# A selective scan: the input of four of 16 states added on TensorE, and C applied by diagonals

## The chip, the cores and the metric

The kernel runs on one core of a Trainium2 chip. The metric is the time of one execution in device microseconds (us). The page and the trace come from one profiled execution. TensorE shows as PE (its weight loads as PEld), VectorE as DVE, ScalarE as ACT, GpSimd as POOL, SyncE's DMA queue as SPq.

## The reference

A decoder layer: a selective state space scan (with convolution, gate and projections), cross attention and a quantized feed-forward net, each with a residual and a layer norm. The change lies in the scan, which runs over eight steps of 128 independent rows, with 512 channels and 16 states:

```python
def step(h, inp):
    d_t, u_t, B_t, C_t = inp
    dA = jnp.exp(d_t[..., None] * A)
    h = dA * h + (d_t * u_t)[..., None] * B_t[:, None, :]
    y = jnp.einsum('bdn,bn->bd', h, C_t)
    return (h, y)
_, ys = jax.lax.scan(step, h0, (deltas, us, Bs, Cs))
y = (ys + us * D[None, None, :]) * _silu(zs)
out = jnp.einsum('md,lbd->lbm', out_proj_w, y)
```

Everything is f32 here. B and C have one value for each row and state, D one for each channel.

## The kernel before

The work is written out by hand for each engine, with semaphores between them. A set-up (about 83 us) makes projections, the convolution, softplus and the skip products: for these, jobs UD multiply blocks of U by `diag_d`, diagonal matrices of D, in true f32 matmuls (128x128 weights, 128 columns, 16 in a burst). Jobs Z are f32 matmuls with 512 columns. Then comes the scan, steps t = 0 to 7 (until about 234 us), and then the attention with the net, on TensorE for the most part.

In the scan the 128 rows lie on partitions, so a state of a step is a tile of 128x512 in `H`. Each of steps 1 to 6 runs through 16 states n:

- GpSimd multiplies delta by A for two states at a time (L1155, a ring of four buffers).
- ScalarE (`decay`, L932) takes the exponential into a PSUM bank of a ring of four (`RING`), once the state four places earlier has left the bank.
- VectorE (`state_decay`, L1355) multiplies the bank by the old state, and `state_add` (L1362) adds B times the input (`step_du`) and writes the new state to `H`. It starts the product of state n+1 ahead of the addition of state n.
- ScalarE (`weigh`, L940) multiplies the state by C, row by row, into one of four slots of `hc` (`WRING`), three states behind the decay (`BEHIND`).
- TensorE (`state_sum`, L574) turns the four 128x128 blocks of the slot (transposes against an identity) and adds them up over states in PSUM bank 4. So the sum over states is done while turning, and Y is kept channel by row.

Ahead of a step's sums `skip_sum` turns the step's skip product into the same bank. It has to wait until `gate` (VectorE, after state 3 of the next step, L1370) has read the last step's Y. After state 3 TensorE projects the gated Y of the step before (`out_proj`), after state 11 it turns x1, the normed result (`turn_x1`). VectorE's `norm1_stats` and `norm1` stand after states 9 and 11. After states 4, 8, 12 and 15 TensorE does a side job, which makes weights of the attention: 22 in all, of the kinds P (four), KV (two), N (four), M (eight: four 128x128 matmuls each) and R (four). ScalarE takes their results some states later (`take_side`, after states 11 and 15 and, of the next step, 2 and 6). Step 7 does without `H` as a target: VectorE (`last_state`, L1398) weighs with C directly into `hc`. When step 7's norm of the token tile before and its decays are through, SyncE loads the attention's rope tables (L423) to where A had been.

Of the kernel before, what the change touches and what calls it, by code (L numbers as in the profile page):

```python
# [21 lines left out]
ACT = mybir.ActivationFunctionType  # L22
AX = mybir.AxisListType

P = 128
T = 8
DM = 256
DI = 512
NST = 16
# [13 lines left out]
RING = 4  # L43
WRING = 4
MRING = 2 * (DM + DQ)
BEHIND = 3
FRESH = 3
PE_SIDE = (4, 8, 12, 15)
ACT_SIDE = (11, 15, NST + 2, NST + 6)
G = 4  # L50
# [27 lines left out]
def decoder_layer(nc, x_fm, x_tiles, wx, wz, conv_w, w_xp, w_dt, b_dt, a_log, d_skip, w_out,  # L78
                  w_q, w_kcq, w_qr, w_kr, w_kckv, w_o, ctx_kv, w_up, w_dn,
                  ident_c, rope_q, rope_kv, had, out, zs_dram, ud_dram, x1_dram, a_dram):  # L80
    with ExitStack() as stack:
# [84 lines left out]
        bcT = x_t[:, :]  # L166
        diag_d = ud_t[:, :].rearrange("p (c n) -> p c n", c=CI)
        wup_raw, wdn_raw = kvT[:, :, :].rearrange("p t n -> p (t n)"), hc[:, 2:4, :].rearrange("p s d -> p (s d)")
        ctx_s = yT[:, :, :].rearrange("p c n -> p (c n)").rearrange("p (t d) -> p t d", t=T)

        Abc = reg_a[:, 0:NST * DI].rearrange("p (n d) -> p n d", n=NST)
# [1 line left out]
        dA = reg_b[:, 8192:12288].rearrange("p (b n d) -> p b n d", b=RING, n=SA)  # L173
        delta_r = reg_c[:, 0:4096].rearrange("p (t d) -> p t d", t=T)
        du_r = reg_c[:, 4096:8192].rearrange("p (t d) -> p t d", t=T)

        ropeq_s = reg_a[:, 0:1536].rearrange("p (w a c n) -> p w a c n", w=2, a=2, c=QC)
        had_s = reg_a[:, 1536:1536 + P]
# [43 lines left out]
        dve_passed = sem("dve_passed"); pool_passed = sem("pool_passed"); act_passed = sem("act_passed"); pe_passed = sem("pe_passed")  # L222

        arg_s = sem("arg_s"); da_s = sem("da_s"); dah_s = sem("dah_s"); h_s = sem("h_s")
        cb_s = sem("cb_s"); hc_s = sem("hc_s"); yl_s = sem("yl_s"); y_s = sem("y_s"); udm = sem("udm")
        st_x = sem("st_x"); st_z = sem("st_z"); st_u = sem("st_u")
        y2_s = sem("y2_s")
# [81 lines left out]
        def work_of(t):  # L309

            return last_work if isinstance(t, int) and t == T - 1 else loop_work

        def last_slot(n):
            return (n + 1 + int(n > FRESH)) % WRING
# [135 lines left out]
        def _(pe):  # L450
# [10 lines left out]
            for j, job in enumerate(jobs):  # L461
# [51 lines left out]
                elif kind == "TU":  # L513
                    once(ld["consts"], 16)
                    for i in range(2):
                        t = 2 * c + i
                        for k in range(CI):
                            last = pe.transpose(o[:, i, k * P:(k + 1) * P], U[:, k, t * P:(t + 1) * P], ident[:, :])
                last.then_inc(pe_job, 1)
            pe.wait_ge(dve_free, freed[("TU", T // 2 - 1)][1])  # L520

            def side_job(j):
# [54 lines left out]
            def skip_sum(t, Y=ps[:, 4, :]):  # L577
# [5 lines left out]
                    last = turn_onto(Y[:, c * P:(c + 1) * P], ud_t[:, c * P:(c + 1) * P], c == 0 and t < T - 1, False)  # L583
                last.then_inc(udm, 1)

            def state_sum(slot, done, count, last_state, Y=ps[:, 4, :], first_state=False):

                pe.wait_ge(done, count)
                for c in range(CI):
                    last = turn_onto(Y[:, c * P:(c + 1) * P], hc[:, slot, c * P:(c + 1) * P], first_state and c == 0, last_state)  # L590
                last.then_inc(y_s, 1)
# [20 lines left out]
            state_sum(0, hc_s, 1, True)  # L612
            pe.wait_ge(ld["wout"], 16)
            for t in range(1, T - 1):
                skip_sum(t)
                for n in range(NST):
                    state_sum((n + 1) % WRING, hc_s, NST * (t - 1) + n + 2, n == NST - 1)
                    if n in PE_SIDE:
                        side_job(per_step * (t - 1) + PE_SIDE.index(n))
                    if n == 3:  # L620
                        out_proj(t - 1)
                    elif n == 11:
                        turn_x1(t - 1)
# [218 lines left out]
        def _(act):  # L842
# [77 lines left out]
            def decay(t, n):  # L920


                act.wait_ge(arg_s, AG * (t - 1) + n // SA + 1)
                if t == T - 1 and n >= RING:
                    act.wait_ge(yl_s, n + 1 - RING)
                else:
                    need(act, h_s, NST * (t - 1) + n + 1 - RING)
                if t == 1 and n == 0:
                    act.wait_ge(act_free, freed[("Z", CI - 1)][1])
                if t == 1 and n == 2:  # L930
                    act.wait_ge(dve_free, freed[("TU", T // 2 - 2)][1])
                act.activation(ps[:, n % RING, :], dA[:, n // SA % RING, n % SA, :], ACT.Exp,  # L932
                               scale=-1.0).then_inc(da_s, 1)

            def weigh(t, n):

                act.wait_ge(h_s, NST * (t - 1) + n + 1)
                need(act, y_s, NST * (t - 1) + n + 2 - WRING)
                s = NST + n
                act.activation(hc[:, (n + 1) % WRING, :], H[:, n, :], ACT.Copy,  # L940
                               scale=bc[:, t, s:s + 1]).then_inc(hc_s, 1)

            squares_of(0)
            skips(0)
# [60 lines left out]
            def scan_step(t, carried):  # L1005
                for n in range(NST):
                    decay(t, n)
                    if n >= BEHIND and t < T - 1:
                        weigh(t, n - BEHIND)
                    elif n < BEHIND and carried:  # L1010
                        weigh(t - 1, NST + n - BEHIND)
                    if t == T - 1 and n == FRESH + 2:
                        fresh_share()
                    if n in ACT_SIDE:
                        take_side(per_step * (t - 1) + ACT_SIDE.index(n))
                    if carried and NST + n in ACT_SIDE:
                        take_side(per_step * (t - 2) + ACT_SIDE.index(NST + n))
                take_x1(t - 1)
# [214 lines left out]
        def _(dve):  # L1233
# [112 lines left out]
            def state_decay(t, n):  # L1346

                dve.wait_ge(da_s, NST * (t - 1) + n + 1)
                E_n = ps[:, n % RING, :]
                if isinstance(t, int) and t == 1:  # L1350

                    dve.scalar_tensor_tensor(E_n, E_n, step_b(0, n), step_du(0), ALU.mult,  # L1352
                                             ALU.mult).then_inc(dah_s, 1)
                    return
                dve.tensor_tensor(E_n, E_n, H[:, n, :], ALU.mult).then_inc(dah_s, 1)  # L1355

            def state_add(t, n):

                dve.wait_ge(dah_s, NST * (t - 1) + n + 1)
                if not (isinstance(t, int) and t == 1):  # L1360
                    dve.wait_ge(hc_s, NST * (t - 2) + n + 2)
                dve.scalar_tensor_tensor(H[:, n, :], step_du(t), step_b(t, n), ps[:, n % RING, :], ALU.mult,  # L1362
                                         ALU.add).then_inc(h_s, 1)

# [28 lines left out]
            def last_state(n):  # L1393

                dve.wait_ge(da_s, NST * (T - 2) + n + 1)
                dve.wait_ge(hc_s, NST * (T - 3) + n + 2)
                dve.wait_ge(y_s, NST * (T - 2) + 1 + n + int(n > FRESH) - WRING + 1)
                dve.scalar_tensor_tensor(hc[:, last_slot(n), :], ps[:, n % RING, :], step_b(T - 1, NST + n), H[:, n, :],  # L1398
                                         ALU.mult, ALU.mult).then_inc(yl_s, 1)

# [10 lines left out]
            def scan_step(t):  # L1411
                state_decay(t, 0)
                for n in range(NST):
                    if n < NST - 1:
                        state_decay(t, n + 1)
                    state_add(t, n)
                    if n == 3:
                        gate(t - 1)
                    elif n == 9:
                        norm1_stats(t - 1)  # L1420
                    elif n == 11:
                        norm1(t - 1)
# [273 lines left out]
```

## Time and profile before

| | us |
|---|---|
| median of three runs | 492.42 (491.68 to 494.4) |
| profiled execution | 493.22 |
| its span, first to last instruction | 491.4 |
| TensorE busy | 415.2 |
| VectorE busy | 390.7 |
| ScalarE busy | 296.8 |
| GpSimd busy | 215.7 |

Busy times are sums over stages with different limits, so the scan is read by itself: by the table of stretches (busy time of each engine between two times, with the clock that was granted to TensorE, 1.00 for 2.4 GHz and 0.50 for 1.2 GHz), by the order of time on single engines, and by who waited for whom. In the order of time a row joins like instructions that follow each other; its start, its busy time and the count stand first. From the start of one row to the start of the next is the time that a group takes when nothing waits. A busy time has the last matmul's way through the array in it, which overlaps the next group. A true f32 matmul leaves two records, a turn one.

### The profile page before, as it was taken

The numbers are of one execution on the slowest core, as the hardware profiler recorded it, in microseconds if no ns is written. First come the engines' busy times: TensorE is split into PE (matmuls) and PEld (weight loads), VectorE is DVE, ScalarE is ACT, GpSimd is POOL, SyncE is SP. The second block draws the span as 40 slices with busy tenths as digits, with TensorE's granted clock in tenths as the row PEclk, the third lists the DMA queues.
The fourth block names the chain that finished last, engine by engine and source line by source line (L and its number), as shares of the span: only waits on it lengthen the run. The fifth ranks groups of instructions, "written<-read, shape, count | busy, mean of one in ns | idle before, by whom it ended". The sixth has DMA issues, their size and how long they took to land.

```text
span 491.4 us, 11537 instructions
## 1 busy us (share of the span) xinstructions
PE 415.2 (84%) x4148; PEld 341.4 (69%) x4148; DVE 390.7 (80%) x744; ACT 296.8 (60%) x699; POOL 215.7 (44%) x157
## 2 busy tenths in 40 slices
PE   4978973587886977969999999999999999999853
PEld 1435532556675866958888888988888888888642
DVE  1876869999999999998466477879878787987675
ACT  3635997899999999995034445453554545354530
POOL 2400003997979797987333332331424233132101
PEclk9989995598798998799999999999999999999955
DMA  8970373116210241101400000000000000000000
GB/s 280 379 302 3 127 226 107 53 43 144 84 53 18 72 158 45 36 29 36 143 1 4 1 13 1 12 13 12 11 0 21 0 11 11 11 11 0 23 1 22
DMA packets 18659, 30.94 MB, mean 63 GB/s; under 512 B 2113, under 2 KB 11713, under 8 KB 17921
## 3 DMA queue, kind: packets, MB, share of 16 engines
q1 hardware_dynamic: 18624, 30.49, 18.8%
q8 instruction: 21, 0.34, 0.3%
q14 instruction: 14, 0.11, 0.1%
HBM read 24.16 MB, written 6.32 MB: 62 GB/s over the span
## 4 chain that ended last, share of the span: by engine, by line
PE 55%; DVE 18%; ACT 14%; issue 9%; DMA 2%; POOL 1%; DVEq 0%; SPq 0%; POOLq 0%; ACTq 0%
PE ps L452 46%; ACT hc L940 5%; PE ps L574 4%; DVE reg_b L1362 4%; PE ps L688 3%; ACT ps L932 3%; DVE ps L1355 2%; DVE ps L1352 2%; DVE reg_b L1296 2%; DVE reg_b L1249 1%; DMA xw<-x_fm 1%; ACT reg_b L912 1%; DMA reg_a<-rope_q 1%; ACT reg_b L1036 1%; POOL reg_b L1155 1%
## 5 line engine op out<-in xcount | busy, mean ns | idle before, releaser
L1155 POOL TENSOR_TENSOR reg_b<-reg_c,reg_a 128x1024 f32<-128x1024 f32 x56 | 130.5, 2373 | 60.4 <-DVE reg_c L1301 60.3
L1178 POOL TENSOR_TENSOR reg_b<-reg_b 128x768 f32<-128x768 f32 x32 | 57.9, 1810 | 117.0 <-DVE reg_b L1434 117.0
L452 PE MATMUL ps<-x1T,Mw 128*128 (+1 forms) x768 | 93.1, 278 | 1.1 <-DVE reg_b L1434 1.1
L452 PEld LDWEIGHTS ps<-x1T,Mw 128*128 128x128 f32 x768 | 88.3, 192 | 3.9 <-DVE reg_b L1434 1.8
L574 PE MATMUL ps<-ident,hc 128*128 128x128 f32 x456 | 72.7, 309 | 16.6 <-ACT hc L940 15.3
L574 PEld LDWEIGHTS ps<-ident,hc 128*128 128x128 f32 x456 | 59.3, 159 | 27.1 <-ACT hc L940 23.9
L940 ACT ACTIVATE hc<-reg_b,bc 128x512 f32<-128x512 f32 x96 | 68.8, 717 | 6.9 <-DVE reg_b L1362 3.4
L1362 DVE SCALAR_TENSOR_TENSOR reg_b<-reg_c,bc,ps 128x512 f32<-128x512 f32 x96 | 70.8, 742 | 0.0
L932 ACT ACTIVATE ps<-reg_b 128x512 f32<-128x512 f32 x112 | 65.8, 592 | 6.9 <-POOL reg_b L1155 6.1
L1355 DVE TENSOR_TENSOR ps<-ps,reg_b 128x512 f32<-128x512 f32 x80 | 55.3, 697 | 0.1
L1036 ACT ACTIVATE reg_b<-ps,small 128x128 f32<-128x128 f32 x128 | 45.3, 373 | 12.8 <-DVE small L1439 12.8
L1160 POOL TENSOR_TENSOR small<-small 128x1 f32<-128x1 f32 x24 | 13.2, 549 | 80.5 <-DVE small L1380 80.5
L452 PE MATMUL ps<-reg_b 64*64 64x128 f32 (+1 forms) x768 | 40.9, 274 | 3.8 <-ACT reg_b L1043 0.5
L1043 ACT ACTIVATE reg_b<-ps 128x512 f32<-128x512 f32 x32 | 19.1, 598 | 40.7 <-PE ps L688 40.7
L452 PEld LDWEIGHTS ps<-reg_b 64*64 64x64 f32 (+1 forms) x768 | 29.4, 134 | 11.2 <-issue 10.2
L1433 DVE TENSOR_TENSOR reg_b<-ps,reg_a 128x768 f32<-128x768 f32 x32 | 30.6, 955 | 7.4 <-PE ps L452 4.8
L452 PE MATMUL ps<-xw,Nw 128*128 128x512 f32 x64 | 30.4, 635 | 6.9 <-DMA xw<-x_fm 6.9
L452 PE MATMUL ps<-reg_b,Nw 64*64 64x128 f32 x1024 | 35.3, 275 | 0.3 <-POOL reg_b L1178 0.2
L1049 ACT ACTIVATE reg_b<-ps 128x256 f32<-128x256 f32 x32 | 12.3, 386 | 33.3 <-PE ps L452 33.3
L452 PEld LDWEIGHTS ps<-reg_b,Nw 64*64 64x64 f32 x1024 | 27.6, 132 | 5.7 <-issue 4.8
L1434 DVE TENSOR_TENSOR reg_b<-ps,reg_a 128x768 f32<-128x768 f32 x32 | 30.3, 948 | 0.0
L452 PE MATMUL ps<-Pw,reg_b 128*128 128x256 f32 x128 | 29.9, 382 | 0.5 <-ACT reg_b L1049 0.5
(150 smaller groups left out, 677.3 us busy)
## 6 DMA issues: line engine op xcount, KB each, us to landing
reg_a<-a_dram SPq DMA_DIRECT2D x4, 1024.0 KB, 7.8
Mw<-w_o SPq DMA_DIRECT2D x1, 2048.0 KB, 15.9
ud_dram<-reg_b SPq DMA_DIRECT2D x4, 512.0 KB, 4.0
zs_dram<-x1T SPq DMA_DIRECT2D x4, 512.0 KB, 3.7
ud_t<-ud_dram SPq DMA_DIRECT2D x8, 256.0 KB, 2.8
zs_t<-zs_dram SPq DMA_DIRECT2D x8, 256.0 KB, 2.7
xw<-x_fm SPq DMA_DIRECT2D x2, 512.0 KB, 5.7
mring<-w_q SPq DMA_DIRECT2D x4, 256.0 KB, 3.8
```

Source lines behind the costliest of these rows:

```text
L452: return pe.matmul(o, l, r, start=start, stop=stop)
L574: return pe.matmul(o, src, ident[:, :], start=start, stop=stop, is_transpose=True, skip_group_check=True)
L932: act.activation(ps[:, n % RING, :], dA[:, n // SA % RING, n % SA, :], ACT.Exp, scale=-1.0).then_inc(da_s, 1)
L940: act.activation(hc[:, (n + 1) % WRING, :], H[:, n, :], ACT.Copy, scale=bc[:, t, s:s + 1]).then_inc(hc_s, 1)
L1036: last = act.activation(prob[:, g % 2, h, :], scores_at(k)[:, h % 2, h // 2, :], ACT.Exp, bias=negm[:, g % 2, h:h + 1], accum_out=sums[:, ...
L1043: act.activation(probT[:, g % 2].rearrange("p h n -> p (h n)"), turned, ACT.Copy).then_inc(pte, 1)
L1155: pool.tensor_tensor(dA[:, g % RING], delta_r[:, bass.ds(t, 1), :].to_broadcast([P, SA, DI]), Abc[:, g * SA:(g + 1) * SA, :], ALU.mult).th ...
L1178: pool.tensor_tensor(rq[:, g % 2].rearrange("p a c n -> p (a c n)"), pc[:, g % 2].rearrange("p a c n -> p (a c n)"), psn[:, g % 2].rearran ...
L1355: dve.tensor_tensor(E_n, E_n, H[:, n, :], ALU.mult).then_inc(dah_s, 1)
L1362: dve.scalar_tensor_tensor(H[:, n, :], step_du(t), step_b(t, n), ps[:, n % RING, :], ALU.mult, ALU.add).then_inc(h_s, 1)
L1433: dve.tensor_tensor(pc[:, g % 2], v, ropeq_s[:, 0], ALU.mult)
L1434: dve.tensor_tensor(psn[:, g % 2, ::-1], v, ropeq_s[:, 1], ALU.mult).then_inc(ropem, 1)
```

## The change

For states 1, 3, 9 and 12 (`ON_PE`) in steps 1 to 6, VectorE makes the product alone. TensorE adds the input onto the product in its PSUM bank (`add_input`): one f32 matmul with a diagonal of B as weights and the step's input, 512 columns, moving. ScalarE makes that diagonal (`diagonal_b`, 128x128) and copies the state from PSUM to `H` (`take_state`). Ahead of the scan TensorE writes each of the three banks concerned once, with the identity.

For all 16 states of these steps C is applied on TensorE: ScalarE makes a diagonal of C (`diagonal`, 128x128 from the identity) in place of the weighed state, and `weighed_sum` multiplies the four blocks of `H` by it, four true f32 matmuls in place of four turns. The 16 diagonals fill all of `hc`. The sums run in another order (`SUM_ORDER`), the projection stands after state 5, and the four additions stand at the step's start (1, 3) and after the sums of states 7 and 10. A state in `H` may be overwritten only when its sum is done, so VectorE's additions, ScalarE's copies and diagonals wait for the sum of the step before (`y_s`). Step 7 starts its weighing when the sums of step 6 that use its slots are done.

```diff
...
+ON_PE = (1, 3, 9, 12)
+SUM_ORDER = (0, 2, 4, 1, 5, 6, 3, 7, 8, 10, 11, 9, 13, 14, 12, 15)
+ADDS = NST - len(ON_PE)
...
+        diag_c = hc[:, :, :].rearrange("p s (i n) -> p (s i) n", n=P)
...
+        diag_b = delta_r[:, 0, :].rearrange("p (i n) -> p i n", n=P)
...
+            pe.wait_ge(cst, 3)
+            pe.wait_ge(act_free, freed[("Z", CI - 1)][1])
+            for b in sorted({n % RING for n in ON_PE}):
+                if b >= 2:
+                    pe.wait_ge(dve_free, freed[("TU", T // 2 - 2)][1])
+                for c in range(CI):
+                    last = mm(ps[:, b, c * P:(c + 1) * P], identb[:, :], identb[:, :], c == 0, c == CI - 1)
+                last.then_inc(set_s, 1)
...
+            def add_input(t, n):
+                pe.wait_ge(dah_s, NST * (t - 1) + n + 1)
+                pe.wait_ge(db_s, on_pe(t, n))
+                pe.matmul(ps[:, n % RING, :], diag_b[:, ON_PE.index(n), :], du_r[:, t, :], start=False, stop=True,
+                          skip_group_check=True).then_inc(pa_s, 1)
+            def weighed_sum(t, n, Y=ps[:, 4, :]):
+                pe.wait_ge(hc_s, NST * (t - 1) + n + 2)
+                new_state(pe, t, n)
+                for c in range(CI):
+                    last = pe.matmul(Y[:, c * P:(c + 1) * P], H[:, n, c * P:(c + 1) * P], diag_c[:, n, :],
+                                     start=False, stop=n == NST - 1, skip_group_check=True)
+                last.then_inc(y_s, 1)
...
             for t in range(1, T - 1):
+                add_input(t, 1)
+                add_input(t, 3)
                 skip_sum(t)
-                for n in range(NST):
-                    state_sum((n + 1) % WRING, hc_s, NST * (t - 1) + n + 2, n == NST - 1)
+                for n in SUM_ORDER:
+                    weighed_sum(t, n)
+                    if n == 7:
+                        add_input(t, 9)
+                    elif n == 10:
+                        add_input(t, 12)
                     if n in PE_SIDE:
                         side_job(per_step * (t - 1) + PE_SIDE.index(n))
-                    if n == 3:
+                    if n == 5:
                         out_proj(t - 1)
                     elif n == 11:
                         turn_x1(t - 1)
...
-                    need(act, h_s, NST * (t - 1) + n + 1 - RING)
+                    u, m = (t, n - RING) if n >= RING else (t - 1, n - RING + NST)
+                    if u >= 1:
+                        new_state(act, u, m)
+                if t == 1 and n < RING:
+                    act.wait_ge(set_s, sum(b <= n for b in {m % RING for m in ON_PE}))
...
-            def weigh(t, n):
-                act.wait_ge(h_s, NST * (t - 1) + n + 1)
-                need(act, y_s, NST * (t - 1) + n + 2 - WRING)
+            def diagonal_b(t, n):
+                i = ON_PE.index(n)
+                need(act, pa_s, on_pe(t - 1, n))
+                act.activation(diag_b[:, i, :], ident[:, :], ACT.Copy, scale=bc[:, t, n:n + 1]).then_inc(db_s, 1)
+            def take_state(t, n):
+                act.wait_ge(pa_s, on_pe(t, n))
+                if t > 1:
+                    act.wait_ge(y_s, summed(t - 1, n))
+                act.activation(H[:, n, :], ps[:, n % RING, :], ACT.Copy).then_inc(ev_s, 1)
+            def diagonal(t, n):
+                if t == 1 and n == 0:
+                    act.wait_ge(y_s, 1)
+                if t > 1:
+                    act.wait_ge(y_s, summed(t - 1, n))
                 s = NST + n
-                act.activation(hc[:, (n + 1) % WRING, :], H[:, n, :], ACT.Copy,
-                               scale=bc[:, t, s:s + 1]).then_inc(hc_s, 1)
+                act.activation(diag_c[:, n, :], ident[:, :], ACT.Copy, scale=bc[:, t, s:s + 1]).then_inc(hc_s, 1)
...
                     decay(t, n)
-                    if n >= BEHIND and t < T - 1:
-                        weigh(t, n - BEHIND)
-                    elif n < BEHIND and carried:
-                        weigh(t - 1, NST + n - BEHIND)
+                    if t < T - 1:
+                        if n + 1 in ON_PE:
+                            diagonal_b(t, n + 1)
+                        diagonal(t, n)
+                        if n - RING + 1 in ON_PE:
+                            take_state(t, n - RING + 1)
...
+                if n in ON_PE:
+                    dve.wait_ge(ev_s, on_pe(t - 1, n))
                 dve.tensor_tensor(E_n, E_n, H[:, n, :], ALU.mult).then_inc(dah_s, 1)
...
-                    dve.wait_ge(hc_s, NST * (t - 2) + n + 2)
+                    dve.wait_ge(y_s, summed(t - 1, n))
                 dve.scalar_tensor_tensor(H[:, n, :], step_du(t), step_b(t, n), ps[:, n % RING, :], ALU.mult,
                                          ALU.add).then_inc(h_s, 1)
...
                 dve.wait_ge(da_s, NST * (T - 2) + n + 1)
-                dve.wait_ge(hc_s, NST * (T - 3) + n + 2)
-                dve.wait_ge(y_s, NST * (T - 2) + 1 + n + int(n > FRESH) - WRING + 1)
+                if n in ON_PE:
+                    dve.wait_ge(ev_s, on_pe(T - 2, n))
+                dve.wait_ge(y_s, NST * (T - 2) + 1 + max(n + int(n > FRESH) - WRING + 1, min(0, n - 2)))
...
                 for n in range(NST):
                     if n < NST - 1:
                         state_decay(t, n + 1)
-                    state_add(t, n)
+                    if n not in ON_PE:
+                        state_add(t, n)
```

TensorE's order in step 2, before, from the skip sum on (`ud_t` the skip product, `hc` the weighed states, `w_out_s` the projection, `x_t` the residual, `Mw` with `ident` a side job KV):

```order
L574 MATMUL ps<-ident,ud_t 128x128 x4
L574 MATMUL ps<-ident,hc 128x128 x16
L452 MATMUL ps<-w_out_s,yT 128x256 x4
L574 MATMUL ps<-ident,x_t 128x128 x2
L574 MATMUL ps<-ident,hc 128x128 x4
L533 MATMUL ps<-ident,Mw 128x128 x4
```

The same place now (`reg_c` with 512 columns the additions, `hc,reg_b` the diagonals of C against the states):

```order
L624 MATMUL ps<-reg_c 128x512 x2
L608 MATMUL ps<-ident,ud_t 128x128 x4
L632 MATMUL ps<-hc,reg_b 128x128 x12
L567 MATMUL ps<-ident,Mw 128x128 x4
L632 MATMUL ps<-hc,reg_b 128x128 x8
L478 MATMUL ps<-w_out_s,yT 128x256 x4
L608 MATMUL ps<-ident,x_t 128x128 x2
L632 MATMUL ps<-hc,reg_b 128x128 x12
L624 MATMUL ps<-reg_c 128x512
L632 MATMUL ps<-hc,reg_b 128x128 x4
```

Two additions stand ahead of the skip sum, the projection has moved behind five sums and a side job, and every sum is a group of matmuls against `reg_b`, the states.

VectorE's order around the gate in the loop over steps, before: the product of state 4, then the addition of state 3, then the gate (`yT`).

```order
L1355 TENSOR_TENSOR ps<-ps,reg_b 128x512 [waits da_s]
L1361 REGISTER_ALU [waits dah_s]
L1362 ISA [waits hc_s]
L1362 SCALAR_TENSOR_TENSOR reg_b<-reg_c,bc,ps 128x512
L1368 REGISTER_ALU [waits y_s]
L1370 TENSOR_TENSOR yT<-ps,zs_t 128x512 [waits op_s,st_z]
```

The same place now, from the addition of state 2 on:

```order
L1440 ISA [waits y_s]
L1440 SCALAR_TENSOR_TENSOR reg_b<-reg_c,bc,ps 128x512
L1424 REGISTER_ALU
L1433 TENSOR_TENSOR ps<-ps,reg_b 128x512 [waits da_s]
L1446 REGISTER_ALU [waits y_s]
L1448 TENSOR_TENSOR yT<-ps,zs_t 128x512 [waits op_s,st_z]
```

The addition of state 3 is gone, so the gate follows the product of state 4 directly, and additions wait for `y_s`, the sums, where they waited for `hc_s`.

## Rows read from the trace of the kernel before

**Rows 1.** The page, busy time of each engine over the span.

```profile
PE 415.2 (84%) x4148; PEld 341.4 (69%) x4148; DVE 390.7 (80%) x744; ACT 296.8 (60%) x699; POOL 215.7 (44%) x157
```

**Rows 2.** Stretches of the scan: steps 2 and 3, and the start of step 1.

```profile
core 0: us, PE busy (x) PEld busy (x) DVE busy (x) ACT busy (x) POOL busy (x), PEclk, DMA share, GB/s
...
114.18:136.26 22.08, 18.53 (x137) 16.12 (x137) 21.89 (x38) 20.53 (x39) 18.88 (x10) 0.77 0.39 105
136.26:158.33 22.07, 16.70 (x144) 13.98 (x145) 21.88 (x38) 21.42 (x44) 19.25 (x10) 0.92 0.13 36
...
91.57:96.00 4.43, 4.43 (x21) 4.43 (x22) 4.43 (x8) 3.38 (x7) 4.43 (x3) 0.50 0.18 59
```

**Rows 3.** VectorE's order of time in step 3: start, busy time, line.

```profile
138.62 0.70 DVE L1355 TENSOR_TENSOR ps<-ps,reg_b 128x512 f32<-128x512 f32 x1
139.22 0.74 DVE L1362 SCALAR_TENSOR_TENSOR reg_b<-reg_c,bc,ps 128x512 f32<-128x512 f32 x1
139.88 0.70 DVE L1355 TENSOR_TENSOR ps<-ps,reg_b 128x512 f32<-128x512 f32 x1
```

**Rows 4.** TensorE's waits in the scan: total us, times, longest.

```profile
PE ps L574 <- DVE yT L1370: 15.0, 5, 6.0
```

**Rows 5.** TensorE's order of time in step 5, nothing waiting.

```profile
180.86 1.91 PE L574 MATMUL ps<-ident,hc 128*128 128x128 f32 x16
182.61 1.89 PE L452 MATMUL ps<-w_out_s,yT 128*128 128x256 f32 x8
...
184.56 0.60 PE L574 MATMUL ps<-ident,hc 128*128 128x128 f32 x4
184.99 1.06 PE L452 MATMUL ps<-mring 128*128 128x128 f32 x8
185.89 2.17 PE L574 MATMUL ps<-ident,hc 128*128 128x128 f32 x16
```

**Rows 6.** TensorE's order of time in the set-up: jobs UD, Z, UD.

```profile
45.15 3.74 PE L452 MATMUL ps<-ud_t,reg_b 128*128 128x128 f32 x32
48.72 7.03 PE L452 MATMUL ps<-xw,Nw 128*128 128x512 f32 x16
55.59 3.73 PE L452 MATMUL ps<-ud_t,reg_b 128*128 128x128 f32 x32
```

**Rows 7.** TensorE's order of time: side jobs P, N and R.

```profile
98.92 1.08 PE L452 MATMUL ps<-Mw 128*64 128x256 f32 x8
...
140.97 1.12 PE L452 MATMUL ps<-Mw 64*64 64x64 f32 x24
...
164.62 1.90 PE L452 MATMUL ps<-mring 128*128 128x64 f32 x16
```

**Rows 8.** Groups of ScalarE in the scan: busy us, mean ns, idle before.

```profile
L940 ACT ACTIVATE hc<-reg_b,bc 128x512 f32<-128x512 f32 x96 | 68.8, 717 | 6.9 <-DVE reg_b L1362 3.4 <-PE ps L574 3.0
L932 ACT ACTIVATE ps<-reg_b 128x512 f32<-128x512 f32 x112 | 65.8, 592 | 6.9 <-POOL reg_b L1155 6.1 <-DVE hc L1398 0.7
...
L986 ACT ACTIVATE Nw<-ps,small 128x128 f32<-128x128 f32 x8 | 2.5, 368 | 0.0
```

**Rows 9.** The scan's end, in order of time: TensorE, VectorE, SyncE's queue, VectorE.

```profile
220.15 5.24 PE L574 MATMUL ps<-ident,hc 128*128 128x128 f32 x32 [0.48 <-ACT hc L940]
...
231.91 0.54 DVE L1390 TENSOR_SCALAR x<-ps,small 128x256 f32<-128x256 f32 x1
...
232.91 0.37 SPq L423 DMA_DIRECT2D reg_a<-rope_q  x1
...
234.51 0.69 DVE L1370 TENSOR_TENSOR yT<-ps,zs_t 128x512 f32<-128x512 f32 x1 [0.75 <-PE ps L574]
...
237.50 0.96 DVE L1433 TENSOR_TENSOR reg_b<-ps,reg_a 128x768 f32<-128x768 f32 x1 [2.30 <-DMA reg_a<-rope_q]
```

**Rows 10.** TensorE's order of time at the start of step 1.

```profile
92.45 3.62 PE L574 MATMUL ps<-ident,hc 128*128 128x128 f32 x16
```

**Rows 11.** TensorE's order of time, start of the attention.

```profile
239.38 2.94 PE L452 MATMUL ps<-x1T,Mw 128*128 128x128 f32 x24 [0.28 <-DVE reg_b L1434]
```

More of the change, by code:

```diff
@@ L224, in decoder_layer @@
         arg_s = sem("arg_s"); da_s = sem("da_s"); dah_s = sem("dah_s"); h_s = sem("h_s")
+        db_s = sem("db_s"); set_s = sem("set_s"); pa_s = sem("pa_s"); ev_s = sem("ev_s")
         cb_s = sem("cb_s"); hc_s = sem("hc_s"); yl_s = sem("yl_s"); y_s = sem("y_s"); udm = sem("udm")
@@ L311, in work_of, with summed, added, on_pe @@
             return last_work if isinstance(t, int) and t == T - 1 else loop_work
+        def summed(t, n):
+            return NST * (t - 1) + SUM_ORDER.index(n) + 2
+        def added(t, n):
+            return ADDS * (t - 1) + sum(m not in ON_PE for m in range(n + 1))
+        def on_pe(t, n):
+            return len(ON_PE) * (t - 1) + ON_PE.index(n) + 1
+        def new_state(eng, t, n):
+            if n in ON_PE:
+                eng.wait_ge(ev_s, on_pe(t, n))
+            else:
+                eng.wait_ge(h_s, added(t, n))
         def last_slot(n):
@@ L1395, in last_state @@
                 dve.wait_ge(da_s, NST * (T - 2) + n + 1)
-                dve.wait_ge(hc_s, NST * (T - 3) + n + 2)
-                dve.wait_ge(y_s, NST * (T - 2) + 1 + n + int(n > FRESH) - WRING + 1)
+                if n in ON_PE:
+                    dve.wait_ge(ev_s, on_pe(T - 2, n))
+                dve.wait_ge(y_s, NST * (T - 2) + 1 + max(n + int(n > FRESH) - WRING + 1, min(0, n - 2)))
                 dve.scalar_tensor_tensor(hc[:, last_slot(n), :], ps[:, n % RING, :], step_b(T - 1, NST + n), H[:, n, :],
```

## The prediction

> **What bounds the kernel now.** The page first: TensorE is busy for 84% of the span and VectorE for 80% [rows 1], which says little, because the kernel has two halves with different limits. The table of stretches, cut at TensorE's skip sums, gives the scan by steps [rows 2]; steps 2 and 3 stand there for the six. VectorE is busy for 21.89 of 22.08 us and 21.88 of 22.07 us. ScalarE has 20.5 and 21.4, GpSimd 18.9 and 19.3, TensorE 18.5 and 16.7, drawn out by waits. So VectorE paces steps 1 to 6. In VectorE's own order of time a decay product starts 0.60 us before the addition behind it, and that 0.66 us before the next product [rows 3]: 1.26 us a state, 20.2 us for 16, which leaves 1.9 us a step for the gate and the layer norm. TensorE is idle for lack of input: its longest waits are those of the skip sum for the gate, 15.0 us in five [rows 4].
>
> **What the change takes away.** Four of 16 additions leave VectorE: 4 x 0.66 = 2.6 us a step, so VectorE alone could do a step in 19.4 us, and GpSimd's 19 us [rows 2] stand close behind. Over six steps that is up to 15.9 us. That is the gain, if nothing else is late.
>
> **What it puts on TensorE.** Three prices are needed, all at the full clock and back to back, from start to start.
> - A state's sum before: four turns (transposes) in 184.99 - 184.56 = 0.43 us [rows 5]; the row of 16 agrees, 1.75 us to the next.
> - A state's sum after: four true f32 matmuls of 128x128 with 128 columns, the state as weights and a diagonal moving. The kernel has this very shape in its set-up: the skip products multiply U by a diagonal of D. Sixteen of them (32 records, two for each matmul) take 48.72 - 45.15 = 3.57 us [rows 6], so 0.223 each and 0.89 us for four. A second place: a weight product of four matmuls in the scan takes 185.89 - 184.99 = 0.90 us [rows 5].
> - An addition of the input: one f32 matmul with 512 columns. Eight of these took 55.59 - 48.72 = 6.87 us [rows 6]: 0.86 us each.
>
> In a step TensorE then has 16 x 0.89 = 14.3 (before 16 x 0.43 = 6.9), additions 4 x 0.86 = 3.4 (before none), the skip sum 0.43, the output projection with its two turns 184.56 - 182.61 = 1.95, the turn of x1 in two turns, half of 0.43, 0.22: 20.3 us. To this come the side jobs, not changed: about 1.0 for one of P or N (1.08 and 1.12 busy, with a tail that overlaps what follows), 1.74 for R (1.90 busy less the same 0.16 by which the rows of M exceed 0.90) [rows 7], 0.90 for M, 0.43 for KV with its four turns. By steps (four P; two KV, two N; two N, two M; two R, two M; three M, one R; one M, one R) 4.0, 2.9, 3.8, 5.3, 4.4 and 2.6: 23.0. A step is so 22.9 to 25.6 us of TensorE work with no gap. That is above the 22.0 of now and far above VectorE's 19.4: **TensorE becomes the bound**, and the four additions bought from VectorE are paid twice, by the additions (3.4 us a step) and, more, by the diagonals of C (7.4 us a step).
>
> A rule on the same point: the Trainium skill, "TensorE: Matmul & The Clock Gate", section Terms, calls transpose mode four times faster for FP32. By it a sum would cost 4 x 0.43 = 1.7 us instead of 0.89. Here rows show a factor of 2 [rows 5, 6]; what that rule would give in time stands among the rivals.
>
> **What can be hidden, and what waits.** Within a step TensorE is rarely short of input. Behind the skip sum it has states 0 and 2 ready, VectorE makes a state in 1.26 us or 0.6 for one of the four, and TensorE takes 0.89 for each plus about 9 us of other work spread between, so it falls behind and stays behind. ScalarE: each 512-wide weighing (717 ns) becomes a 128-wide diagonal, nearest row the 128x128 copy with a scale, 368 ns [rows 8]. With 16 decays at 592, 20 diagonals at 368, four evictions of states at about 592 and some 3 us of jobs that is 22 us without overlap; before, the same count gives 24 where 20.5 to 21.4 were busy. So I take about 19 us for ScalarE, by the row nearest to a diagonal. Were a diagonal as dear as the weighing that it replaces (717), ScalarE would come to 29 by that count and to some 25 with the overlap, level with TensorE; were it free, nothing would change, since TensorE is the bound.
>
> The place to look at is the end of a step. The gate waits for the last sum, and the skip sum waits for the gate; now two additions (1.7 us) stand between, which were not there to fill the 15 us [rows 4]. But ScalarE evicts the job behind state 12 before decay 3: eviction 0.59, decay 0.59, diagonal 0.37, decay 0.59, then VectorE's product 0.70 [rows 3] and the gate 0.69 [rows 9] are 3.5 us, and with the hand-overs I take 4.0, against the last sum, a job and the two additions on TensorE, 0.89 + 1.0 + 1.7 = 3.6. I take 0.4 us of wait at each of the four boundaries whose last job is short: 1.6 us. Bounds: 0 where every hand-over is short (R is long enough to cover it), 1 us each where ScalarE also evicts the two-part N.
>
> The new wait on ScalarE, state 1's eviction on its addition, has decay 5 queued behind it; that holds VectorE until about 2.9 us into the step, when TensorE is still at states 0 and 2 with a skip sum ahead. The diagonals wait for the sum of the step before, which is done by then.
>
> The clock. At the start of step 1 the granted clock is 0.50, so 1.2 GHz, until 96 us [rows 2]; before it the engine had been idle. There 16 turns took 3.62 us where 1.91 stand later [rows 5, 10]. TensorE does in 4.4 us what it could in 2.2: +2.2 us for step 1. Later steps hold few gaps, so I take 2.4 GHz; bounds are 0 and another 4.4 us.
>
> **The sum.** 6 x 20.3 + 23.0 = 144.8; less the first step's two early additions, which lie before its skip sum, 1.7; plus 2.2 and 1.6: 146.9 us from the first skip sum. That starts at about 91.2 (the gate stands behind two additions fewer, but GpSimd paces those first states), so the last sum of step 6 ends at 238.1. Before, it ended at 220.15 + 0.66 = 220.8 [rows 9]. So +17.3. Behind it, the rope tables are loaded once the norm of token tile 6 is through: norm 231.91, load 232.91, used at 237.50, 16.7 us after the last sum [rows 9]. In the new order VectorE starts the last step while two sums are open and is not held by GpSimd, which had time to fill its four buffers: 12 products at the 0.66 of an addition [rows 3] and the 1.9 of gate and norm make 9.8, so the norm is done 9.9 us after the last sum, load half a microsecond later, 4.6 to its use: 15.0, so -1.7. In all +15.6. The profiled execution took 493.22 us for its span of 491.4; it becomes 508.8, and as it stood 0.8 above the median of the runs, the time is **508 us**.
>
> Bounds: the sum at 0.98 for four matmuls, as 24 records in 2.94 us at the start of the attention would have it [rows 11], adds 96 x 0.09 = 8.4; boundaries and clock at their worst add about 4. All of the small terms at zero take off 3.8, and a shorter tail 1.5. So 503 to 520.
>
> **Rivals.**
> - The gain arrives: TensorE's two-record matmuls of different sums overlap better than in the set-up, VectorE stays the bound, and a step takes 19.4 us: 493 - 6 x 2.6 = 477 us. For that a TensorE step of 20.3 + 3.8 (the mean of the jobs) has to fall to 19.4, so a sum from 0.89 to 0.60 us. At 0.76 the step is the 22 us of now, and from there on the change is slower; the set-up's diagonals at 0.89 speak against both. Chance 0.03, and 0.03 for the level case (490 to 495).
> - TensorE bound, but the boundary is bare: gate 2 us late at five boundaries, and each gap drops the clock as in step 1, 5 x (2 + 2.2) = +21, so about 529. For it: the clock now falls in the middle of the scan, mean 0.77 in the second step [rows 2]. Against: the gaps that did so are those the two additions fill. Chance 0.12.
> - A sum at four times a turn (the mechanism of transposes in one pass against four): 96 x (1.72 - 0.89) = +80, about 588. Chance 0.02, since the set-up rows show half of that price. The rule of the Trainium skill named above, in "TensorE: Matmul & The Clock Gate" (Terms), is this case.
> - The forecast: 0.80.
>
> **How the numbers follow.** Predicted 508; the range 503 to 520 holds most of the forecast and the mild part of the bare boundary. 0.5% (2.5 us) is about what a measurement of this kernel can tell from no change. Faster 0.03, same 0.03, slower 0.94.
>
> **What would show it.** In the profile after: TensorE busy nearly without a break from 92 to 238 us with a granted clock near 1.00; sums of four matmuls (eight records) every 0.89 us; VectorE some 4 us idle a step, its waits naming TensorE's sums; skip sums 23 to 26 us apart. The step that fails if the time comes out at 493 or lower is the price of a sum; if at 525 and more, the boundary.

## The result, and the profile after

The changed kernel takes **507.93 us** (median of four runs, 507.38 to 509.97) against 492.68 for the kernel before beside it: a ratio of 1.0317, with a 95% interval from 1.0275 to 1.0359. It is slower by about 15 us, as predicted (508). The profiled execution took 508.12 us for a span of 505.9; the prediction had put it at 508.8.

The page of after, busy time of each engine over the span. TensorE went from 84% to 91% and VectorE from 80% to 75% [rows 1]:

```profile
PE 458.8 (91%) x4592; PEld 379.8 (75%) x4592; DVE 378.8 (75%) x720; ACT 287.5 (57%) x747; POOL 216.3 (43%) x157
```

The six steps of the scan, cut at TensorE's skip sums (the last one ends with its last sum); steps 2 and 3 answer to [rows 2]:

```profile
core 0: us, PE busy (x) PEld busy (x) DVE busy (x) ACT busy (x) POOL busy (x), PEclk, DMA share, GB/s
90.25:115.63 25.38, 25.38 (x186) 20.42 (x185) 20.39 (x33) 17.90 (x42) 23.43 (x11) 0.99 0.14 38
115.63:139.65 24.02, 23.92 (x209) 20.81 (x208) 19.80 (x33) 19.50 (x48) 19.33 (x9) 1.00 0.42 110
139.65:164.83 25.18, 24.83 (x217) 21.73 (x217) 20.01 (x33) 20.11 (x52) 19.30 (x9) 1.00 0.12 33
164.83:190.57 25.74, 25.74 (x200) 23.53 (x201) 19.99 (x33) 18.63 (x45) 19.31 (x9) 1.00 0.25 73
190.57:215.83 25.26, 24.97 (x193) 22.45 (x191) 19.99 (x33) 19.53 (x46) 19.30 (x9) 1.00 0.19 63
215.83:237.33 21.50, 21.50 (x174) 20.29 (x175) 16.28 (x27) 15.50 (x36) 17.20 (x9) 1.00 0.13 38
```

Read the first two columns: TensorE is busy for all but at most 0.35 us of each step, at a clock of 0.99 to 1.00, and the five full steps last what it takes, 24.0 to 25.7 us where steps 2 and 3 were 22.1. VectorE, which had filled the steps before, has 19.8 to 20.4. The bound has moved from VectorE to TensorE.

TensorE's order of time in after (start, busy time, line, operation; several instructions in a row stand as one): the sums, then the boundary between steps 4 and 5.

```profile
188.80 1.94 PE L624 MATMUL ps<-reg_c 128*128 128x512 f32 x4
190.57 0.60 PE L608 MATMUL ps<-ident,ud_t 128*128 128x128 f32 x4
191.01 2.85 PE L632 MATMUL ps<-hc,reg_b 128*128 128x128 f32 x24
193.70 1.06 PE L478 MATMUL ps<-mring 128*128 128x128 f32 x8
```

Three sums (24 records) take 193.70 - 191.01 = 2.69 us, 0.897 each, where the prediction had 0.89 and the turns before had 0.43 [rows 5]. Two additions take 190.57 - 188.80 = 1.77, predicted 1.72, and the skip sum is still 0.44.

The waits in after (who waits, for whom: total us, times, longest). The skip sum's wait for the gate was 15.0 us [rows 4]:

```profile
PE ps L608 <- DVE yT L1448: 0.6, 2, 0.3
ACT reg_b L1006 <- PE ps L624: 26.8, 16, 4.3
DVE ps L1433 <- ACT ps L992: 20.5, 25, 2.5
```

TensorE waits for almost nothing. In the other two rows ScalarE's evictions of the four states (L1006) wait for TensorE's additions, the decays (L992) stand behind them in ScalarE's queue, and VectorE's products wait for those: TensorE's pace, handed on through ScalarE.

The scan's end in after, beside [rows 9]: the last sums, the norm, the load of the rope tables and their use.

```profile
232.72 4.63 PE L632 MATMUL ps<-hc,reg_b 128*128 128x128 f32 x40
247.38 0.54 DVE L1468 TENSOR_SCALAR x<-ps,small 128x256 f32<-128x256 f32 x1
248.38 0.37 SPq L449 DMA_DIRECT2D reg_a<-rope_q  x1
252.79 0.96 DVE L1513 TENSOR_TENSOR reg_b<-ps,reg_a 128x768 f32<-128x768 f32 x1 [2.12 <-DMA reg_a<-rope_q]
```

The last sum ends at 232.72 + 4.63 = 237.35; before it was 220.8. The tables are used 15.4 us behind it, predicted 15.0 (before 16.7). Of the span's 14.5 us more, the stretch up to this use has 252.79 - 237.50 = 15.3, so all of the loss lies ahead of it. It is not the scan's start, which came 1.3 us earlier than before (skip sum at 90.25 for 91.57): the loss is in the steps.

### The profile page after: what moved, and what is told of

Read it like the earlier page. It is cut to its first block, busy times and chain, and to the rows that moved or that the text cites. A ratio compares the mean times of both kernels' runs of the same rounds, so it can differ in the third digit from the quotient of the medians.

```text
span 505.9 us, 12479 instructions
## 1 busy us (share of the span) xinstructions
PE 458.8 (91%) x4592; PEld 379.8 (75%) x4592; DVE 378.8 (75%) x720; ACT 287.5 (57%) x747; POOL 216.3 (43%) x157
## 4 chain that ended last, share of the span: by engine, by line
PE 76%; DVE 9%; issue 6%; ACT 5%; DMA 2%; POOL 0%; DVEq 0%; SPq 0%; POOLq 0%; ACTq 0%
PE ps L478 49%; PE ps L632 17%; PE ps L624 4%; PE ps L744 3%; PE ps L608 2%; DVE reg_b L1372 1%; DVE reg_b L1325 1%; DMA xw<-x_fm 1%; ACT reg_b L968 1%; ACT reg_b L1112 1%; DMA reg_a<-rope_q 1%; ACT reg_b L974 1%; DVE reg_b L1514 1%; PE ps L785 1%; DVE reg_c L1382 1%
## 5 line engine op out<-in xcount | busy, mean ns | idle before, releaser
L632 PEld LDWEIGHTS ps<-hc,reg_b 128*128 128x128 f32 x768 | 90.4, 192 | 7.4 <-issue 6.0
L632 PE MATMUL ps<-hc,reg_b 128*128 128x128 f32 x768 | 94.2, 276 | 0.0
L992 ACT ACTIVATE ps<-reg_b 128x512 f32<-128x512 f32 x112 | 66.2, 594 | 6.6 <-DVE hc L1477 2.7
L1440 DVE SCALAR_TENSOR_TENSOR reg_b<-reg_c,bc,ps 128x512 f32<-128x512 f32 x72 | 52.7, 739 | 0.0
L1015 ACT ACTIVATE hc<-ident,bc 128x128 f32<-128x128 f32 x96 | 37.9, 395 | 0.8 <-PE ps L608 0.8
```

The source lines that it names most:

```text
L632: last = pe.matmul(Y[:, c * P:(c + 1) * P], H[:, n, c * P:(c + 1) * P], diag_c[:, n, :], start=False, stop=n == NST - 1, skip_group_check= ...
L1015: act.activation(diag_c[:, n, :], ident[:, :], ACT.Copy, scale=bc[:, t, s:s + 1]).then_inc(hc_s, 1)
```

## Experiments

Each changes the kernel after; the edits of 5, 8 and 9 are shown against the experiment that they build on. The edits are cut to what matters. Step times are from the same cut at the skip sums; ratios are to the kernel before in the same batch (491.65 us for the first four, 493.6 for the next three, 493.47 for the last two), with 95% intervals.

**1. The diagonals of C alone.** VectorE adds all 16 inputs again, and the sums stand in their natural order.

```
-ON_PE = (1, 3, 9, 12)
-SUM_ORDER = (0, 2, 4, 1, 5, 6, 3, 7, 8, 10, 11, 9, 13, 14, 12, 15)
+ON_PE = ()
+SUM_ORDER = tuple(range(NST))
...
-                add_input(t, 1)
-                add_input(t, 3)
                 skip_sum(t)
...
-                    if n == 7:
-                        add_input(t, 9)
-                    elif n == 10:
-                        add_input(t, 12)
```

> C by diagonals for all 16 states, all 16 additions back on VectorE, sums in natural order. Theory (the change is slower by the TensorE work it adds, which makes TensorE the bound): without the four additions a step has 24.1 - 3.4 = 20.7 us of TensorE work, VectorE needs 22.1, so VectorE paces again: 490 to 498 us, TensorE idle 1 to 2 us a step at the skip sum. Rival (not the work but the new waits set the pace: states in H and diagonals wait for the sums of the step before): those waits are all still there, so 503 us or more.

Measured 509.33 us, ratio 1.0353 (1.0299 to 1.0407): a miss of over 10 us, and the number that the rival had. Steps 3 and 4 by engines, a wait, and the order of time that explains it (the gate ahead of step 3, the projection, the norm statistics):

```profile
143.74:169.00 25.26, 22.75 (x209) 21.72 (x209) 21.95 (x38) 17.09 (x42) 19.23 (x10) 0.94 0.12 32
169.00:193.43 24.43, 22.42 (x192) 22.02 (x192) 21.94 (x38) 16.29 (x38) 19.18 (x10) 1.00 0.28 79
```

```profile
DVE small L1447 <- PE ps L608: 14.3, 6, 3.4
```

```profile
143.01 0.68 DVE L1442 TENSOR_TENSOR yT<-ps,zs_t 128x512 f32<-128x512 f32 x1
152.19 1.89 PE L478 MATMUL ps<-w_out_s,yT 128*128 128x256 f32 x8
154.34 0.43 DVE L1447 BATCH_NORM_STATS2 small<-ps 128x6 f32<-128x256 f32 x1 [3.12 <-PE ps L608]
```

No engine fills these steps: TensorE has 22.4 to 22.8 us of 24.4 to 25.3, VectorE 21.9. The work goes round in a ring. Gate, then on TensorE the dearer sums of the first states and the projection, done about 11 us after the gate; then VectorE's norm statistics, which stand in its order behind state 9 and hold the later states back for 3.1 us; then the next gate. My theory had counted the engines one by one and not this ring; the rival had waits set the pace, but other ones, those for the last step's sums, and no wait of VectorE or ScalarE in these steps names them.

**2. The additions alone.** ScalarE weighs the states and TensorE turns them as before, in natural order; TensorE adds four inputs.

```
...
-                    weighed_sum(t, n)
-                    if n == 7:
+                    state_sum((n + 1) % WRING, hc_s, NST * (t - 1) + n + 2, n == NST - 1)
+                    if n == 5:
                         add_input(t, 9)
-                    elif n == 10:
+                    elif n == 8:
                         add_input(t, 12)
...
+                    if n >= BEHIND and t < T - 1:
+                        weigh(t, n - BEHIND)
+                    elif n < BEHIND and carried:
+                        weigh(t - 1, NST + n - BEHIND)
```

> The four additions on TensorE, but C as before: ScalarE weighs the state, TensorE turns it. TensorE then has some 17 us of work a step. Theory: VectorE could do 19.4 to 20 us, but ScalarE, which in the changed kernel is busy for 19 to 20 us a step with diagonals of 0.395, gets 16 weighings of 0.717 instead, 5 us more: 24 to 25 us a step, ScalarE bound, 499 to 509 us. Rival (the additions alone are a gain, and only the diagonals of C spoil it): VectorE paces at 19.4 to 20 us a step, 477 to 483 us.

Measured 509.37 us, ratio 1.0328 (1.0251 to 1.0406), at the upper end of what I expected. Step 5 by engines, and the two large waits:

```profile
190.76:215.76 25.00, 19.49 (x130) 14.97 (x128) 19.97 (x33) 24.47 (x46) 19.32 (x9) 1.00 0.20 64
```

```profile
PE ps L608 <- ACT hc L1013: 21.4, 32, 1.2
DVE ps L1435 <- ACT ps L992: 26.0, 31, 3.1
```

ScalarE is busy for 24.47 of 25.00 us, and both others wait for it. So the additions bring nothing here without the diagonals, which relieve ScalarE; and the diagonals are what fills TensorE.

**3. Half of each sum.** If TensorE's work bounds the change, less of it must give time back at once. Two of the four matmuls of each sum are left out, so half of Y lacks the scan; every wait stays.

```
-                for c in range(CI):
+                for c in range(CI // 2):
                     last = pe.matmul(Y[:, c * P:(c + 1) * P], H[:, n, c * P:(c + 1) * P], diag_c[:, n, :],
```

> The changed kernel, with two of four matmuls of every weighed sum left out, so that two of four channel blocks of Y lack the scan; every wait is kept. Theory (TensorE work): a step loses 16 x 0.45 = 7.1 us of TensorE work, 17 are left, and the step falls to what VectorE and GpSimd need, 19.4 to 20 us: 477 to 486 us, faster than the kernel before. Rival (waits and hand-overs): 503 us or more.

Measured 482.34 us, ratio 0.9808 (0.9743 to 0.9874). Step 3 by engines:

```profile
131.02:151.31 20.29, 18.36 (x153) 14.73 (x153) 19.51 (x34) 19.90 (x53) 18.75 (x9) 1.00 0.13 40
```

With the sums at half price the step is 20.3 us, VectorE (19.5) and ScalarE (19.9) stand nearest to it, and the gain that the four additions could bring shows: 9 us below the kernel before. The sums' price on TensorE is the cause of the loss.

**4. Two states on TensorE in place of four.**

```
-ON_PE = (1, 3, 9, 12)
+ON_PE = (1, 9)
+SUM_ORDER = (0, 2, 3, 1, 4, 5, 6, 7, 8, 10, 11, 9, 12, 13, 14, 15)
...
-                add_input(t, 3)
...
-                    elif n == 10:
-                        add_input(t, 12)
```

> The changed kernel with the input of two states (1 and 9) added on TensorE instead of four. Theory: TensorE work falls by 2 x 0.86 = 1.7 us a step to 22.4 and stays the bound (VectorE 20.7): 508 - 6 x 1.7 = 498, between 495 and 500 us. Rival (waits): no change within 3 us of 508, or, if the additions on TensorE were a help by themselves, slower than 508.

Measured 503.72 us, ratio 1.0218 (1.0156 to 1.0279), some 4 us above the stretch that I expected. Step 3, and the first 6 us of step 1:

```profile
142.21:165.62 23.41, 23.12 (x213) 20.98 (x213) 20.88 (x35) 18.14 (x48) 19.32 (x10) 1.00 0.13 35
```

```profile
93.58:99.58 6.00, 6.00 (x31) 6.00 (x32) 6.00 (x10) 4.59 (x12) 6.00 (x4) 0.54 0.12 44
```

Steps 2 to 5 fell as expected, by 1.5 to 2.1 us (two additions are 1.72). The miss is step 1, which took 26.1 us, its first six at a mean clock of 0.54, and a scan that began 3 us later in this execution (skip sum at 93.58 us for 90.25).

**5. Experiment 1 with the projection early**, behind state 1, to open the ring.

```
-                    if n == 5:
+                    if n == 1:
                         out_proj(t - 1)
```

> E1 (C by diagonals alone) with one change: the projection of the step before stands after state 1's sum instead of state 5's. New theory for E1: VectorE keeps the pace, but it stands still for some 3 us a step at the norm's statistics after state 9, since the projection on TensorE, behind six dearer sums, ends 9 to 10 us after the gate, and the gate of the next step is some 14 us behind the statistics on VectorE; this ring of gate, sums, projection, norm and gate makes 24 us. Then the projection ends 4 to 5 us after the gate, before VectorE is there, and a step is VectorE's 22.1: 490 to 497 us. Rival (TensorE's own work, 20.7 us, with the 2 us gaps at the skip sum is the bound in E1): the gaps stay, 505 us or more.

Measured 500.88 us, ratio 1.0166 (1.011 to 1.0222): in between. Step 3 by engines, and two of the waits that are left:

```profile
139.31:162.87 23.56, 21.40 (x209) 20.37 (x209) 22.09 (x38) 17.04 (x43) 20.73 (x11) 1.00 0.11 34
```

```profile
ACT x1T L1029 <- PE ps L658: 13.7, 6, 2.5
DVE ps L1427 <- ACT ps L986: 4.2, 5, 1.2
```

The wait of the statistics is gone. From the skip sum of step 1 to that of step 7 it is now 141.3 us, where experiment 1 had 147.3 and the kernel before 133.7: the ring was real and held 6.0 of the 13.6 us that the steps had lost. The other 3 us between the two experiments lie ahead of the scan, which began at 91.36 us here and at 94.51 there. Of the 7.6 us that are left, step 1 has 3.3 (25.9, its first six at a mean clock of 0.57). In the other steps ScalarE's copy of x1 waits for its turn on TensorE and holds the decays behind it; that is read from the waits and was not tried alone.

**6. The changed kernel with the projection early**, behind state 2: does the ring pace it too?

```
-                    if n == 5:
+                    if n == 2:
                         out_proj(t - 1)
```

> The changed kernel with the projection after the second sum of a step (state 2) instead of the sixth (state 5). Theory of the prediction (TensorE's work is the bound there): the work is the same, 505 to 511 us. Rival (the ring by way of the projection, as in E1, is what paces the changed kernel too): the ring gets 4 us shorter, 485 to 497 us.

Measured 509.01 us, ratio 1.0305 (1.024 to 1.037). Step 3:

```profile
143.46:168.63 25.17, 24.83 (x217) 21.73 (x217) 19.89 (x33) 20.07 (x52) 19.34 (x9) 1.00 0.11 33
```

25.17 us and 24.83 busy, to a hundredth what it was, and steps 2 to 6 all agree to 0.02 us. TensorE is full there, and the place of the projection does not matter; the ring is excluded as the cause in the changed kernel. Only step 1 is longer, 26.43 us for 25.38 (see the clock, below).

**7. Half of the diagonals.** The odd states are summed by diagonals, the even ones weighed by ScalarE and turned as before; two states on TensorE; the projection behind state 1.

```
-ON_PE = (1, 3, 9, 12)
+ON_PE = (1, 9)
...
+DIAG = (1, 3, 5, 7, 9, 11, 13, 15)
...
+                    if n in DIAG:
+                        weighed_sum(t, n)
+                    else:
+                        state_sum(TURN.index(n) % 2, wg_s, weighed(t, n), False)
```

> A mixture: the input of two states (1, 9) is added on TensorE, C goes by diagonals for the eight odd states and is weighed by ScalarE and turned for the eight even ones, projection after state 1. By the prices found: TensorE 15.0 + 8 x 0.46 = 18.7 us a step, ScalarE 20 to 21, GpSimd 19.3, VectorE 20.7 and the bound: 1.2 to 1.4 us less a step than before, 482 to 489 us. Rival: ScalarE, which holds decays, diagonals, weighings, evictions and the jobs, is late in between, a step stays at 22 us or more: 492 to 500 us.

Measured 491.68 us, ratio 0.9962 (0.9936 to 0.9988): above the expected stretch by over 2 us. Step 3, and VectorE's wait for decays in steps 2 to 6:

```profile
138.24:160.71 22.47, 19.91 (x181) 17.19 (x181) 21.30 (x36) 20.63 (x49) 20.11 (x10) 1.00 0.12 36
```

```profile
DVE ps L1453 <- ACT ps L998: 3.2, 7, 1.2
```

TensorE is down to 19.9 (24.83 less eight times the 0.47 between a sum and its turns, less two additions, makes 19.3); VectorE is again the fullest engine, at 21.3, as two additions relieve it by only 1.3 us. But it waits for ScalarE's decays, and the step is no shorter than the 22.07 of before, as the rival had it with ScalarE late in between.

**8. The same with a third state (3) on TensorE.**

```
-ON_PE = (1, 9)
-SUM_ORDER = tuple(range(NST))
+ON_PE = (1, 3, 9)
+SUM_ORDER = (0, 1, 2, 4, 3) + tuple(range(5, NST))
...
+                add_input(t, 3)
```

> E7 (C by diagonals for the odd states, the even ones weighed) with state 3's input on TensorE too. If E7's steps are held by VectorE's own work, 0.6 to 0.66 us less a step: 487 to 490 us. If ScalarE's hand-overs hold it (a further diagonal of B and a further eviction, 0.8 us, on ScalarE), no gain or a loss: 491 to 497 us.

Measured 490.69 us, ratio **0.9956** (0.9934 to 0.9978), just between the two. It has the lowest ratio with whole sums, 0.4% below the kernel before, about as little as can be told from none, and not to be told from experiment 7. Step 4:

```profile
156.59:179.30 22.71, 21.90 (x166) 19.50 (x167) 20.62 (x34) 19.97 (x43) 20.02 (x10) 1.00 0.29 83
```

All four engines stand at 20 to 22 of 22.7 us: work moved between them has little left to give. Of the 3 us between this execution and the profiled one of before, the steps hold only 1.3 (132.4 us from the skip sum of step 1 to that of step 7, for 133.7); the rest lies ahead of the scan and behind it.

**9. Experiment 7 with the diagonals elsewhere**, weighed states away from the step's end.

```
-DIAG = (1, 3, 5, 7, 9, 11, 13, 15)
+DIAG = (1, 5, 7, 9, 11, 13, 14, 15)
```

> E7 with another choice of the eight diagonals: 1, 5, 7, 9, 11, 13, 14, 15, so that none of the last states of a step is weighed while ScalarE starts the next step. If VectorE's 0.85 us a step of waits for ScalarE's decays in E7 come from those weighings, 3 to 5 us less than E7: 487 to 490 us; if not, 490 to 494 us as E7.

Measured 495.62 us, ratio 1.0062 (1.0036 to 1.0087): the wrong way. VectorE's wait for decays and ScalarE's for turns in steps 2 to 6, where experiment 7 had 3.2 us in seven of the first and none of the second; then, from step 3, a weighing and VectorE's product behind it:

```profile
DVE ps L1453 <- ACT ps L998: 8.5, 12, 1.4
ACT hc L1020 <- PE ps L614: 4.6, 5, 1.3
```

```profile
141.13 0.72 ACT L1020 ACTIVATE hc<-reg_b,bc 128x512 f32<-128x512 f32 x1 [0.78 <-PE ps L614]
142.37 0.70 DVE L1453 TENSOR_TENSOR ps<-ps,reg_b 128x512 f32<-128x512 f32 x1 [0.96 <-ACT ps L998]
```

Three weighed states (2, 3 and 4) now follow one another through two slots. State 4's weighing waits until TensorE has turned state 2 out of its slot, the next decay stands behind it in ScalarE's queue, and VectorE's product waits for that. This is read from the waits; a kernel with more slots was not tried.

## Why the prediction was right, point by point

- **The bound.** Right, by the stretches of after and by experiment 3: with half of TensorE's sums the time was some 26 us below the changed kernel's, and an earlier projection (experiment 6) gave nothing.
- **The prices.** A sum 0.897 us for 0.89, an addition 0.885 for 0.86, a diagonal on ScalarE 395 ns for 368. The set-up's rows [rows 6] held in the scan to 1 and 3%. The rival of a sum at four times a turn (588 us) is out: 0.897 / 0.43 = 2.1. The Trainium skill, "TensorE: Matmul & The Clock Gate" (Terms), calls transpose mode four times faster for FP32; the factor of 2.1 of these shapes does not agree with it.
- **The steps.** Gap-free work was put at 143.1 us (24.3, 23.2, 24.1, 25.6, 24.7, 21.2); measured 147.1, predicted with all terms 146.9. Two terms inside were wrong and nearly cancel; that the sum came within 0.2 us is luck.
- **The clock, mis-sized.** I added 2.2 us for a low clock at the start of step 1. In this execution it was paid ahead of the step: the two early additions ran at the low level, and the clock rose as the skip sum ran. Two stretches, then the order of time on TensorE, then the gate:

```profile
86.00:90.25 4.25, 3.83 (x4) 1.01 (x5) 4.25 (x8) 4.16 (x11) 4.25 (x3) 0.50 0.10 39
90.25:96.00 5.75, 5.75 (x48) 5.10 (x48) 5.75 (x9) 5.38 (x13) 5.75 (x3) 0.97 0.14 46
```

```profile
86.42 4.00 PE L624 MATMUL ps<-reg_c 128*128 128x512 f32 x4 [1.82 <-issue]
90.25 0.81 PE L608 MATMUL ps<-ident,ud_t 128*128 128x128 f32 x4
90.89 1.28 PE L632 MATMUL ps<-hc,reg_b 128*128 128x128 f32 x10
...
89.51 0.68 DVE L1448 TENSOR_TENSOR yT<-ps,zs_t 128x512 f32<-128x512 f32 x1
```

 The additions took 90.25 - 86.42 = 3.83 us at 0.50 (1.2 GHz) where 1.77 stand later. It cost nothing, since the gate that the skip sum waits for was itself done only at 89.51 + 0.68 = 90.19. The skip sum took 0.64 us for 0.43, so 0.2 us of the term is left. How much is paid differs from one execution to the next. Experiment 6 has the same two additions ahead, but in its execution the clock was low for longer:

```profile
93.01:98.76 5.75, 5.75 (x34) 5.50 (x34) 5.75 (x9) 5.37 (x13) 5.75 (x3) 0.78 0.17 46
```

 Its step 1 took 1.05 us more than this one, so some 1.3 us of the term. Experiment 4, with one early addition, needed 26.1 us for step 1, though it has two additions less to do in it.
- **Sums beside narrow jobs, left out.** In place of the clock, 4.0 - 1.5 = 2.5 us appear elsewhere (147.1 less 143.1, and less the boundaries below). A sum next to a job with operands 64 wide (P, N) is longer. Here is one behind a P, then one between two:

```profile
103.04 1.08 PE L478 MATMUL ps<-Mw 128*64 128x256 f32 x8
104.05 1.16 PE L632 MATMUL ps<-hc,reg_b 128*128 128x128 f32 x8
105.05 1.02 PE L624 MATMUL ps<-reg_c 128*128 128x512 f32 x2
...
110.69 1.08 PE L478 MATMUL ps<-Mw 128*64 128x256 f32 x8
111.70 1.16 PE L632 MATMUL ps<-hc,reg_b 128*128 128x128 f32 x8
112.79 1.08 PE L478 MATMUL ps<-Mw 128*64 128x256 f32 x8
```

 The first takes 105.05 - 104.05 = 1.00 us and the second 112.79 - 111.70 = 1.09 where 0.897 is usual, so 0.10 for each side. The eight jobs P and N have 14 such sides in the scan, which makes 1.4 us, by the same reading of every sum. Of the rest, skip sums of up to 0.64 us for 0.43 hold 0.5 (0.2 of it the low clock), jobs N at 1.05 for 1.0 hold 0.2, sums behind R (0.95) 0.2, and the tail of the last sum's busy time 0.2.
- **The boundary.** Second-pair additions to skip sum take 1.83, 2.09, 2.23, 1.77 and 2.17 us for a gap-free 1.72: 1.5 us in all, predicted 1.6, and almost none behind the long R (1.77), as predicted. Behind P there was little too (1.83). The stretch from ScalarE's eviction to the gate's end, taken as 4.0 us, is 4.06 at the end of step 2 (135.54 to 138.92 + 0.68):

```profile
135.54 0.39 ACT L1057 ACTIVATE Nw<-ps 128x256 f32<-128x256 f32 x1 [1.23 <-PE ps L478]
138.92 0.68 DVE L1448 TENSOR_TENSOR yT<-ps,zs_t 128x512 f32<-128x512 f32 x1
```

 The bare boundary (529) is out: the clock stayed at 1.00.
- **ScalarE and VectorE.** ScalarE has 17.9 to 20.1 us in the full steps, predicted about 19. VectorE is idle for 4 to 6 us a step, predicted some 4, but its waits name ScalarE's decays, not TensorE's sums. The cause is the same, one link further back.
- **The start.** The skip sum of step 1 came at 90.25 us for the 91.2 that I had taken. With the same work ahead of it, it came at 93.01 in experiment 6, so here too the closeness is luck.
- **The gain.** The diagonals alone (experiment 1) and the additions alone (2) each cost 16 to 18 us and both together 15: parts of a change need not add up. The additions alone run into ScalarE, the diagonals alone into a ring, both into TensorE.

## What to carry to other kernels

Price the moved work on the engine that receives it, by the same shape elsewhere in the same trace, and sum that engine's step without gaps: if the sum is above the present step, the saving elsewhere never arrives. Where several engines stand within a tenth of each other, moving work shows only up to the next one, and half of a change may be better than all of it (experiments 7 and 8). When no engine is full and the step still grows, look for a ring through in-order queues, and test it by moving one instruction group.

## What the runs showed of the hardware

- A true f32 matmul of 128x128 with 128 columns costs 0.223 to 0.225 us in the set-up [rows 6], in the scan of before [rows 5] and in that of after (0.897 / 4); a turn costs 0.109 (16 in 1.75 [rows 5]).
- Next to a matmul group with operands 64 wide, such a group of four took 0.10 us more on each side (1.00 and 1.09 us for 0.897).
- TensorE's first work in the scan, after a pause, ran at a granted clock of 0.50 (1.2 GHz). Whether that costs time depends on what is put there, and differs between executions: over the first 5.75 us of step 1 the mean clock was 0.97 in after and 0.78 in experiment 6, with the same two additions ahead.
- The scan's start differs by some 3 us between executions: the first skip sum stands at 90.25 us in after and at 93.01 in experiment 6, which do the same up to there. Profiled executions should be compared by their steps.
